# Building the node-by-edge one-hot of a graph attention kernel with a three-row matmul and a ScalarE Relu

## The reference, cut to what matters

```
q = (edge_state @ Wq + bq).reshape(N, H, D)
k = (edge_state @ Wk + bk).reshape(N, H, D)
v = (edge_state @ Wv + bv).reshape(N, H, D)
e = (angle_emb @ We).reshape(-1, H, D)
k_e = k[src] + e
v_e = v[src] + e
alpha = jnp.einsum('ehd,ehd->eh', q[dst], k_e) / jnp.sqrt(jnp.float32(D))
m = jax.ops.segment_max(alpha, dst, num_segments=N)
a = jnp.exp(alpha - m[dst])
z = jax.ops.segment_sum(a, dst, num_segments=N)
attn = a / z[dst]
out = jax.ops.segment_sum(attn[:, :, None] * v_e, dst, num_segments=N)
...
x_r = edge_state @ Wskip + bskip
beta = jax.nn.sigmoid(jnp.concatenate([out, x_r, out - x_r], axis=-1) @ Wbeta)
out = beta * x_r + (1.0 - beta) * out
...
return edge_state + jax.nn.relu(out)
```

## Time and profile before

| what | us |
|---|---|
| median of the runs (2530.57 to 2537.65) | 2535.12 |
| profiled execution, first to last instruction (its span) | 2124.7 |
| what the median has beyond that span | 410.4 |
| start of the span to the first gather | 79.8 |
| first gather to last gather | 1962.2 |
| last gather to the end of the span | 82.7 |

### The profile page before, as it was taken

The page is one execution under the profiler, slowest core; times in us unless marked ns, Lnnn a source line. Parts: engine busy times, 40 slices in busy tenths (PEclk is TensorE's granted clock), DMA queues, the critical chain, the costliest instruction groups (busy, mean ns, idle before and its releaser), DMA issues. The chain is left out here.

```text
span 2124.7 us, 43320 instructions
## 1 busy us (share of the span) xinstructions
PE 1580.3 (74%) x10903; PEld 1429.2 (67%) x10903; DVE 1807.1 (85%) x3704; ACT 1121.3 (53%) x3755; POOL 1502.4 (71%) x1586
## 2 busy tenths in 40 slices
PE   7678788778776777777776777777777777877763
PEld 5577777668676666666675776667666767767652
DVE  6687787788878888888888898898898999999985
ACT  1154445445445545555555555566555665666656
POOL 0377777777777777777777777777777777777750
PEclk9898899998999999999999989999999999899985
DMA  8887787777777777777777777777777777777741
GB/s 297 280 246 233 233 240 235 236 233 236 222 215 212 218 216 214 222 211 218 221 215 225 216 223 217 222 226 221 215 223 225 226 224 228 224 226 219 228 128 36
DMA packets 298207, 467.63 MB, mean 220 GB/s; under 512 B 49766, under 2 KB 192826, under 8 KB 297862
## 3 DMA queue, kind: packets, MB, share of 16 engines
q1 hardware_dynamic: 222552, 259.24, 39.7%
q0 software_dynamic: 75408, 205.58, 33.7%
HBM read 413.96 MB, written 50.66 MB: 219 GB/s over the span
## 5 line engine op out<-in xcount | busy, mean ns | idle before, releaser
L742 POOL DMA_INDIRECT kv<-kv_tab,src_all x1498 | 1425.4, 952 | 480.9 <-issue 443.4
L851 PE MATMUL e_ps<-we,ea 128*128 128x128 f32 x3136 | 472.2, 301 | 278.4 <-DVE kve L1437 271.8
L851 PEld LDWEIGHTS e_ps<-we,ea 128*128 128x128 f32 x3136 | 417.7, 208 | 324.5 <-DVE kve L1437 175.6
L1437 DVE TENSOR_TENSOR kve<-kv,e_ps 128x768 f32<-128x768 f32 (+1 forms) x392 | 421.6, 1084 | 214.8 <-DMA kv<-kv_tab,src_all 214.0
L1095 ACT ACTIVATE dist_en<-iota_n,neg_rel 128x128 bf16<-128x128 f32 x1568 | 500.0, 396 | 46.3 <-issue 46.3
L1119 ACT ACTIVATE wt_ps<-logit,used_b 128x64 f32<-128x64 f32 x196 | 62.3, 318 | 831.3 <-issue 692.0
L969 PE MATMUL sum_ps<-wv,hot_en 128*128 128x136 f32 x3136 | 466.4, 303 | 11.8 <-DVE wv L1487 4.6
L969 PEld LDWEIGHTS sum_ps<-wv,hot_en 128*128 128x128 f32 x3136 | 429.7, 209 | 31.9 <-issue 31.9
L864 PE MATMUL q_ps<-q_win,hot_ne 128*128 128x128 f32 x3136 | 420.6, 292 | 0.9 <-DMA q_win<-q_tab 0.9
L864 PEld LDWEIGHTS q_ps<-q_win,hot_ne 128*128 128x128 f32 x3136 | 407.3, 210 | 1.2 <-DMA q_win<-q_tab 1.2
L1458 DVE TENSOR_REDUCE logit<-prod 128x64 f32<-128x1024 f32 x196 | 239.2, 1220 | 19.4 <-issue 0.4
(11 more groups left out here) (144 smaller groups left out, 1237.9 us busy)
## 6 DMA issues: line engine op xcount, KB each, us to landing
ea<-eaT SPq DMA_DIRECT2D x196, 512.0 KB
row_b<-rel_row SPq DMA_DIRECT2D x196, 256.0 KB
q_win<-q_tab SPq DMA_DIRECT2D x392, 64.0 KB
kv<-kv_tab,src_all POOLq DMA_INDIRECT x1498
sum_tab<-sums SPq DMA_DIRECT2D x391, 59.5 KB
kv_tab<-tab_buf SPq DMA_DIRECT2D x33, 384.0 KB, 3.7
logit<-sum_tab SPq DMA_DIRECT2D x49, 136.0 KB
xt_buf<-xT SPq DMA_DIRECT2D x33, 192.0 KB, 4.0
```

The costliest lines, as they stand in the source:

```text
L742: pool.indirect_dma_start(out=head_rows(q) if u == t == 0 else kv[:, s, t, :], out_offset=None, in_=kv_tab[:, :], in_offset=bass.IndirectO ...
L851: mm = pe.matmul(e_ps[u][:, t * P:(t + 1) * P], ea[:, par, (u * TILES_G + t) * P:(u * TILES_G + t + 1) * P], we[:, :], start=True, stop=True)
L1437: dve.tensor_tensor(kve[:, s, a:TILES_G, :, :], kv[:, s, a:TILES_G, :].rearrange("p t (a c) -> p t a c", a=2), e4[:, a:TILES_G, :, :].to_b ...
```

## The change

The comparison on DVE and the broadcast load go. The one-hot is now 1 at node position n and edge position r where 1 - (n - r)^2 is positive, that is Relu(1 - n^2 + 2nr - r^2). The middle part is a matmul over three rows of bf16: the left operand `node3` holds 2n, -1 and -1, the right one `rel3` holds r and r^2 in two bf16 parts (`rel_hi`, `rel_lo`, whose sum is exact). 1 - n^2 is the bias `near_b` of the Relu on ACT.

- New on PE: `nearness`, one matmul per group into `q_ps` (the bank in which `q_spread` later writes its result), behind each `edge_part`. It waits for `products` of the group that used the bank before.
- New on ACT: `node_one_hot`, one Relu of 512 per group out of `q_ps` into `hot_ne`, between `unit_part` and `weights`. `hot_ne` shrinks to two group buffers.
- `q_spread` now waits for that Relu; `weights` no longer waits for `hotne_ok`.
- SP loads three rows of 1024 (`rel3`, 6 KB) a pair and stores three tables in place of one after round 10 of the table stage.
- New setup: on ACT two Squares of 98 by 2048, on DVE the difference `rel_lo` of 98 by 2048 and four short instructions.

```diff
-            def node_one_hot(q, par, i, reuse=True):
-                dve.wait_ge(row_ld[par], 16 * (i + 1))
-                if reuse:
-                    dve.wait_ge(q_ok, 2 * q - 2)
-                dve.tensor_tensor(hot_ne[:, 2 * par:2 * par + 2, :].rearrange("p u e -> p (u e)"), row_b[:, par, :],
-                                  row_id.to_broadcast([P, PAIR]), ALU.is_equal).then_inc(hotne_ok, 2)
...
+            def nearness(q, par, u, i):
+                g = 2 * q + u
+                if u == 0:
+                    pe.wait_ge(row_ld[par], 16 * (i + 1))
+                if q:
+                    pe.wait_ge(prod_ok, g - 1)
+                pe.matmul(q_ps[u][:, :], node3[:, :], rel3[:, par, u * EDGES_G:(u + 1) * EDGES_G], start=True, stop=True
+                          ).then_inc(near_ok, 1)
...
+            def node_one_hot(g):
+                act.wait_ge(near_ok, g + 1)
+                if g >= 2:
+                    act.wait_ge(q_ok, g - 1)
+                act.activation(hot_ne[:, g % 2, :], q_ps[g % 2][:, :], ACT.Relu, bias=near_b[:, :]).then_inc(hotne_ok, 1)
...
                     for u in range(2):
                         edge_part(q + 1, 1 - par, u, i + par, False)
+                        nearness(q + 1, 1 - par, u, i + par)
...
-                act.wait_ge(hotne_ok, min(2 * q + 4, GROUPS))
...
                 unit_part(q)
+                if q + 1 < PAIRS:
+                    for u in range(2):
+                        node_one_hot(2 * q + 2 + u)
...
-                    sp.wait_ge(hotne_ok, 2 * q - 2)
-                sp.dma_start(row_b[:, q % 2, :], rel_row[:, q * PAIR:(q + 1) * PAIR].to_broadcast([P, PAIR])
-                             ).then_inc(row_ld[q % 2], 16)
+                    sp.wait_ge(near_ok, 2 * q - 2)
+                sp.dma_start(rel3[:, q % 2, :], rel_tab[:, q * PAIR:(q + 1) * PAIR]).then_inc(row_ld[q % 2], 16)
...
-                    sp.wait_ge(row_cast, 1)
-                    sp.dma_start(rel_row.rearrange("one (p j) -> (one p) j", j=2 * PAIR), rel_rows[:, :]
-                                 ).then_inc(rel_st, 16)
+                    for k, rows in enumerate((rel_rows[:, :], rel_hi, rel_lo)):
+                        sp.wait_ge(row_cast, k + 1)
+                        sp.dma_start(rel_tab[k:k + 1, :].rearrange("one (p j) -> (one p) j", j=2 * PAIR), rows
+                                     ).then_inc(rel_st, 16)
```

More of the change, by code:

```diff
@@ L248, in build @@
         g_put = sb("g_put", [P, 1], I32)
+        rel_sq = kve[0:PAIRS // 2, 0:2, :, :, :].rearrange("p s t a c -> p (s t a c)")
+        rel_hi = hot_en[0:PAIRS // 2, 0:2, :, :].rearrange("p s t n -> p (s t n)").bitcast(BF16)
+        rel_lo = hot_en[0:PAIRS // 2, 2:4, :, :].rearrange("p s t n -> p (s t n)").bitcast(BF16)
         dst_rows = logit[0:PAIRS // 2, 0:2 * PAIR].bitcast(I32)
@@ L351, in build @@
         denom_ok = sem("denom_ok")
-        rowid_ok = sem("rowid_ok")
+        square_ok = sem("square_ok")
+        node3_ok = sem("node3_ok")
+        near_ok = sem("near_ok")
         sums_ok = sem("sums_ok")
@@ L988, in _ @@
             with pe.If(grouped):
+                pe.wait_ge(node3_ok, 2)
                 for u in range(2):
+                    nearness(0, 0, u, 0)
                     edge_part(0, 0, u, 0, True)
                 for u in range(2):
-                    q_spread(0, 0, u, 0, True)
+                    q_spread(0, 0, u, 0)
                 for u in range(2):
                     edge_part(1, 1, u, 0, False)
+                    nearness(1, 1, u, 0)
                 biases_made()
@@ L1247, in _ @@
             with act.If(grouped):
+                act.wait_ge(rel_st, 16 * NEAR_K)
+                act.wait_ge(node3_ok, 2)
+                for u in range(2):
+                    node_one_hot(u)
                 for q in range(ROUND):
@@ L1587, in unit_part, with step @@
                     mix(u)
-            def step(q, par, i, first=None, ahead=True):
+            def step(q, par, i, first=None):
                 reuse = first is None or first >= 2
@@ L1602, in step @@
                 weighted(q, par, reuse)
-                if ahead:
-                    node_one_hot(q + 2, par, i + 1)
                 unit_part(q)
             with dve.If(grouped):
-                dve.tensor_copy(row_id, part_id[:, :]).then_inc(rowid_ok, 1)
-                dve.wait_ge(rowid_ok, 1)
-                for q in range(2):
-                    node_one_hot(q, q, 0, False)
                 for q in range(ROUND):
@@ L1632, in _ @@
                 for q in range(PAIRS - ROUND, PAIRS):
-                    step(q, q % 2, q // 2, ahead=q + 2 < PAIRS)
+                    step(q, q % 2, q // 2)
                     if q == PAIRS - 3:
```

40 lines of the change are left out of this document (26 added, 14 removed).

## The result

The changed kernel takes 3046.39 us, the median of 4 runs between 3037.34 and 3059.12; the kernel before took 2534.80 us beside it (4 runs, 2530.57 to 2537.65). The ratio is 1.2024, with a 95% interval of 1.1988 to 1.2061: 512 us slower, where the prediction had 2 us.

What follows compares the result with a forecast made beforehand. POOL's uninterrupted gathers, 10.05 us a pair, were taken as the bound, with DVE close behind. Loop 0, head +4 and tail -2 us sum to +2 on 2535.12 us: 2537 us at 76%, range 2524 to 2547 us.

Steps and rivals of the forecast that it cites:

- The sum's base: The 410.4 us between profile span and timed median, taken as unchanged, so that 2535.12 + 2 gives 2537 us.
- Part one: Pair loop: POOL's gathers never stop at 10.05 us a pair, so taking 237.9 us off DVE changes 0 us.
- its wait for gathers: DVE in the pair loop: its wait for gathers to land would rise by roughly 100 us or more.
- Its wait for the exponential: DVE in the pair loop: waits about 0.6 us a step for the later exponential, where it didn't before.
- Rival one: Pair loop: PE - ACT - PE becomes the bound if its mean exceeds 10.05 us; 2551 or 2584 us; 14%.
- Its signs: Pair loop: gathers waiting over 0.3 us for `kve`, ACT idle before the Relus, PE idle before `q_spread`.
- the hand-overs: Signals between engines in the PE - ACT - PE loop, put at 0.3 us within its 9.3 us.
- Its 9.3 us: PE - ACT - PE loop, exponential to next exponential: 3.1 to the sums, sums, `edge_part`, `nearness`, Relu and hand-overs.
- Part two: Up to the first gather: DVE's table setup and two more stores on SP, +4 us, ends 0 and 6.8.
- Part three: After the last gather: DVE has caught up and begins the last pair earlier, -2 us, ends 0 and -4.
- Sum on the second kind: Whole kernel: 0 + 4 - 2 = +2 us, span 2126.7 us for 2124.7.
- The rule on relu: Skill's advice of VectorE over ScalarE for a relu; by it alone a pair would be 0.2 us slower.

Runs made afterwards that it cites:

- first kind: Jobs in which the unchanged kernel before takes 2531 to 2597 us, at a granted clock of 0.78 (four jobs).
- the first job: The kernel before, unchanged, profiled anew: 2600.32 us, ratio 1.0005; its job also ran the changed kernel with later Relus (1.2816) and the kernel before with added matmuls (1.0280).
- second kind: Jobs in which the unchanged kernel before takes 2119 to 2121 us, at a granted clock of 0.92 (three jobs); the prediction's profile is of this sort.
- The second and the seventh job: Second: matmul order (1.0437), one-hot on ScalarE (1.0001), half the node sums (0.9884, changed kernel 1.1248). Seventh: kernel before without POOL's wait for `q_spread`, 2120.15 us.

## Why the prediction was wrong

**The sum's base failed.** "No row shows what makes the 410.4 us between the span and the median; I take it as unchanged." That is the step that failed. In every run here span and time are within 2.1 us. The 410 us were not something around the span but the pauses of POOL in other executions, of the first kind (the first job's 474 us over that span, against 479 us of pauses). The profile of the prediction is of the second kind. The other terms were worked out for the second kind, so each is set against both kinds below.

**Part one, "POOL never stops", 0 us: right on the second kind, some 507 us short on the first.** (The 200 and 199 gathers that it reads are 200 and 200 in the earlier trace rows, which changes nothing.) On the second, gathers went from 87.7 to 2045.4, 1957.7 us as against 1962.2, VectorE's busy time is 1591.9 us (forecast 1572), and its wait for gathers rose from 214.0 to 268.9 us, half of the 100 expected. Its wait for the exponential is 154.1 us in 192 times, 0.8 us a step where 0.6 was forecast. The chain over the Relu was there and stayed under the gathers' pace. On the first kind POOL was already the one that waits, and each link that the change put between a signal of TensorE and the one that POOL waits for lengthened its pause.

**Rival one named the right loop, at the wrong price.** Its signs came (gathers that wait, ScalarE idle before the Relus, TensorE before `q_spread`) but it was priced at 2551 to 2584 us. The term that failed is the hand-overs, put at 0.3 us all together: on the first kind a signal from TensorE that comes late in a row of gathers waits for the row's end, with a pause of 5.0 us as the result. Its 9.3 us don't name `q_spread` either, which the change puts behind the Relu and ahead of the running maximum and the next sums. But the way from the exponential to the next sums, which contains its end, took 3.0 us in the median of all steps on the second kind, as the 3.1 us assumed, and 4.5 us on the first.

**Part two, +4 us.** The first gather came at 77.5 to 85.3 us in the thirteen traces without the new setup, at 79.6 in the median, and at 81.7 to 88.6 in the seven with it, at 84.2 in the median. So 4.6 us where 4 was forecast, as the difference of two wide groups; single pairs of traces differ by anything from -4 to 11 us.

**Part three, -2 us.** On the second kind the last pair's first sum begins 10.6 us after the last gather in the changed kernel, as worked out (10.7); it was 12.7 before, and no trace of this kind with all gathers and without the change has less than 12.4. From the last gather to the end, 82.7 us before and 2126.3 - 2045.4 = 80.9 us now agree too, but other traces without the change have 79.8 to 84.7 us, so that this number alone shows little.

**Sum on the second kind:** +3.7 us measured (+1.7 to +5.9), +2 forecast. The prediction's working holds for the kind of execution whose profile it read, though 3.7 and 2 us are too near each other and to the scatter to confirm its parts one by one. The two numbers beside it, 2124.7 and 2535, said that this was not the kind that was timed.

**The rule on relu.** The Trainium skill (ScalarE: Activation LUTs, Rules for kernel authors) advises VectorE and not ScalarE for a relu. No run here shows a loss by it: the 0.2 us a pair that the prediction put beside it would be 39 us, and on the second kind the whole change costs 3.7; on the first, 407 us more on ScalarE and 1.2 us a pair less on VectorE leave the time as it is.

## What to carry to other kernels

Where a profile's span and the timed median differ by more than a few us, take the profile to be of another regime than the timed runs: forecast the change in both, and ask first which engine could stop in the one that isn't shown. A step that turns a finished operand into a round trip TensorE - ScalarE - TensorE should have other matmuls between its two ends, here two lines in another order for 393 us on the first kind. And look at what stands between a late signal and the engine that issues gathers: in the first kind of execution its pause sets the pace of the whole loop.

## What the runs showed of the hardware

- The same kernel takes 2120 us in some jobs and 2531 to 2597 in others, with all its runs within 0.7% of one another in each job. Whether that belongs to the chip or to its condition at the time isn't told. The second and the seventh job bear the same chip number and had 2534.49 and 2119.00 us; if that is one and the same chip, it is the condition. Every execution here was recorded with its span, so none shows whether the recording has a part in it.
- In the slower ones, signals of TensorE come late, 99 of 100 within 7.4 us of its modelled ends in the kernel before, in bursts of which half begin 1.62 to 1.85 us after the last of a row of gathers. Inside rows of gathers, none of the kernel before's and 6 of the changed kernel's 461 that came on time did so from the fifth gather on. The signals of VectorE that were recorded inside the rows came on time (686 in the kernel before), but three in five of its signals have no event in that trace. What holds TensorE's isn't known, and the rule has exceptions: in the changed kernel 182 of 242 pauses contain a late signal, and of its events that come over 0.3 us late 280 of 944 come while gathers go on.
- The mean granted clock is no measure of the time: on the second kind it was 0.92 with all matmuls and 0.67 with half of the full-width ones left out, at 2120 and 2116 us; on the first kind 0.78 and 0.62, at 2531 and 2527 us.
